# Metaformer kernel, first stage: in every second pair of rows ScalarE puts the mask into the gate and VectorE takes the pair's product in one operation

## The reference, cut to what matters

```python
m = mask[..., None]
a = _ln_fp32(act, ln_in_w, ln_in_b)
left  = m * (a @ left_proj_w.T  + left_proj_b)  * sigmoid(a @ left_gate_w.T  + left_gate_b)
right = m * (a @ right_proj_w.T + right_proj_b) * sigmoid(a @ right_gate_w.T + right_gate_b)
t = einsum('bikc,bjkc->bijc', left, right)
t = _ln_fp32(t, ln_c_w, ln_c_b)
out = (t @ out_proj_w.T + out_proj_b) * sigmoid(a @ gating_w.T + gating_b)
```

## Time and profile before

| | |
|---|---|
| median of 3 runs | 995.27 us (994.14 to 995.28) |
| the profiled execution's own time | 994.61 us |
| its span, first to last instruction | 992.8 us |
| mean granted TensorE clock over the span | 0.969 |
| busy over the span: TensorE matmul | 921.4 us (93%) |
| VectorE | 819.0 us (82%) |
| GpSimd | 660.1 us (66%) |
| ScalarE | 449.4 us (45%) |
| the first stage's products (L838) | 512 of them, started between 28.5 and 215.5 us |
| the first stage's sigmoids (L492) | 128 of them, started between 25.5 and 214.0 us |

### The profile page before, as it was taken

The page is one execution under the profiler, slowest core; times in us unless marked ns, Lnnn a source line. Parts: engine busy times, 40 slices in busy tenths (PEclk is TensorE's granted clock), DMA queues, the critical chain, the costliest instruction groups (busy, mean ns, idle before and its releaser), DMA issues.

```text
span 992.8 us, 22220 instructions
## 1 busy us (share of the span) xinstructions
PE 921.4 (93%) x7352; PEld 524.8 (53%) x7352; DVE 819.0 (82%) x2945; ACT 449.4 (45%) x842; POOL 660.1 (66%) x632
## 2 busy tenths in 40 slices
PE   4788999979999867999999999999999999999987
PEld 3566666758888544444444444444444444444432
DVE  4899999971122568999999999999999999999993
ACT  1555555641111123454554555545555455454543
POOL 5898888813322213877778777787777777877765
PEclk9999999989999955999999999999999999999999
DMA  7587777997997112324334333343342433433332
GB/s 195 179 283 246 265 264 261 311 351 235 306 300 228 32 32 76 107 90 125 114 100 128 98 117 120 96 128 103 112 127 88 128 112 104 125 97 120 102 93 73
DMA packets 119395, 153.15 MB, mean 154 GB/s; under 512 B 10486, under 2 KB 76278, under 8 KB 117238
## 3 DMA queue, kind: packets, MB, share of 16 engines
q1 hardware_dynamic: 118150, 151.32, 49.3%
q10 hardware_dynamic: 1136, 0.46, 0.2%
HBM read 67.33 MB, written 50.33 MB: 119 GB/s over the span
## 4 chain that ended last, share of the span: by engine, by line
PE 52%; DVE 35%; issue 6%; POOL 3%; DMA 3%; ACT 1%; SPq 0%; DVEq 0%; ACTq 0%; POOLq 0%
PE b_m L777 14%; PE ein L665 11%; DVE zb L1001 8%; DVE stage L838 7%; PE ring L764 6%; PE pr_a L628 4%; PE gt L702 4%; DVE bst L825 4%; PE gt L686 3%; PE b_d L686 3%; PE b_d L746 2%; DVE x2t L1020 2%; PE b_m L769 2%; DVE bst_x L1052 2%; DVE bst_t L899 2%
## 5 line engine op out<-in xcount | busy, mean ns | idle before, releaser
L442 POOL TENSOR_TENSOR zb<-bcs,x2d 128x512 f32<-128x512 f32 x256 | 326.3, 1277 | 154.3 <-ACT bcs L549 154.0
L549 ACT ACTIVATE bcs<-ring 128x512 f32<-128x512 f32 x256 | 152.7, 597 | 243.4 <-PE ring L764 243.3
L777 PE MATMUL b_m<-zb,w_exp 128*64 128x512 f32 x1024 | 253.7, 611 | 0.1
L1001 DVE TENSOR_TENSOR zb<-ring,x2d 128x512 f32<-128x512 f32 x256 | 175.5, 685 | 20.7 <-PE ring L764 18.6
L838 DVE SCALAR_TENSOR_TENSOR stage<-pr_a,mt,sig_a 128x128 f32<-128x128 f32 x512 | 148.4, 427 | 11.5 <-ACT sig_a L492 10.3
L628 PE MATMUL pr_a<-w_proj,xts 64*128 64x256 f32 x1024 | 138.2, 400 | 16.3 <-DVE stage L838 15.7
L777 PEld LDWEIGHTS b_m<-zb,w_exp 128*64 128x64 f32 x1024 | 61.0, 136 | 143.4 <-issue 118.3
L764 PE MATMUL ring<-wt,sel 64*128 64x512 f32 x512 | 127.5, 494 | 8.4 <-DVE zb L1001 4.4
L427 POOL TENSOR_TENSOR tn<-t_all,rr 128x512 f32<-128x512 f32 x64 | 85.3, 1333 | 52.0 <-DVE rr L929 27.4
L628 PEld LDWEIGHTS pr_a<-w_proj,xts 64*128 64x128 f32 x1024 | 95.5, 190 | 44.4 <-issue 26.1
L492 ACT ACTIVATE sig_a<-pr_a 128x512 f32<-128x512 f32 x128 | 76.4, 597 | 73.0 <-PE pr_a L628 72.8
(11 more groups left out here) (132 smaller groups left out, 1440.9 us busy)
## 6 DMA issues: line engine op xcount, KB each, us to landing
left_right_scratch<-stage SPq DMA_DIRECT2D x16, 2048.0 KB, 7.6
x2d<-x2t SPq DMA_DIRECT2D x256, 128.0 KB, 2.9
chunk<-left_right_scratch SPq DMA_DIRECT2D x24, 1024.0 KB, 9.1
xc<-in_x SPq DMA_DIRECT2D x64, 256.0 KB, 3.3
out<-outc SPq DMA_DIRECT2D x64, 256.0 KB, 2.1
chunk<-left_right_scratch SPq DMA_DIRECT2D x12, 384.0 KB, 7.6
chunk<-left_right_scratch SPq DMA_DIRECT2D x8, 192.0 KB, 5.9
chunk<-left_right_scratch SPq DMA_DIRECT2D x4, 256.0 KB, 8.0
```

The costliest lines, as they stand in the source:

```text
L442: pool.tensor_tensor(zb[:, tile_buffer(u, m), :], bcs[:, n % 2, :], x2d[:, u % 2, m % 2, :], ALU.mult)\
L549: act.activation(bcs[:, n % 2, :], ring[:, m % 2, :], ACT.Copy).then_inc(bcast_out, 1)
L777: ins = pe.matmul(b_m[rows[t], :], w_exp[:, ep, :], zb[:, tile_buffer(u, 2 * ep + t), :], start=ep == 0, stop=ep == EP - 1, skip_group_che ...
L1001: dve.tensor_tensor(zb[:, tile_buffer(u, m), :], ring[:, m % 2, :], x2d[:, u % 2, m % 2, :], ALU.mult).then_inc(z_dve, 1)
```

## The change

`act_masks(p)` is true for odd p. In such a pair ScalarE, after the sigmoid, waits for it on a new semaphore and then multiplies the mask into the gate in place, with four ACTIVATEs (Copy, with a per-partition scale read from `mt`), one for each row and q, of 128 elements. Only then is the gate announced to VectorE, which takes the product of projection and masked gate for the whole pair in one TENSOR_TENSOR of 512 elements in place of four SCALAR_TENSOR_TENSORs of 128. Even pairs are as before. The number of announcements on every semaphore that others wait for is unchanged.

```diff
+def act_masks(p):
+
+    return p % 2 == 1
...
-        sig_ready = sem("sig_ready"); lr_done = sem("lr_done"); stored = [sem("stored0"), sem("stored1")]
+        sig_ready = sem("sig_ready"); sig_raw = sem("sig_raw"); lr_done = sem("lr_done"); stored = [sem("stored0"), sem("stored1")]
...
                 if p >= PAIR_RING:
                     act.wait_ge(lr_done, p - PAIR_RING + 1)
-                act.activation(sig_a[:, k, :, :, :], pr_a[:, k, :, :].rearrange("p q (r c) -> p q r c", r=PAIR)[:, :, :, 2 * C:4 * C],
-                               ACT.Sigmoid).then_inc(sig_ready, 1)
+                gate_in = pr_a[:, k, :, :].rearrange("p q (r c) -> p q r c", r=PAIR)[:, :, :, 2 * C:4 * C]
+                ins = act.activation(sig_a[:, k, :, :, :], gate_in, ACT.Sigmoid)
+                if act_masks(p):
+                    ins.then_inc(sig_raw, 1)
+                    act.wait_ge(sig_raw, p // 2 + 1)
+                    for r in range(PAIR):
+                        for q in range(Q):
+                            row = p * PAIR + r
+                            ins = act.activation(sig_a[:, k, q, r, :], sig_a[:, k, q, r, :], ACT.Copy, scale=mt[:, row:row + 1, q])
+                ins.then_inc(sig_ready, 1)
...
                 if n >= 2 and p * PAIR % ROWS == 0:
                     dve.wait_ge(stored[n % 2], n // 2 * 16)
+                if act_masks(p):
+                    row = p * PAIR % ROWS
+                    ins = dve.tensor_tensor(
+                        stage[:, n % 2, :, :, row:row + PAIR].rearrange("p q c r -> p q r c"),
+                        pr_a[:, p % PAIR_RING, :, :].rearrange("p q (r c) -> p q r c", r=PAIR)[:, :, :, 0:2 * C],
+                        sig_a[:, p % PAIR_RING, :, :, :], ALU.mult)
+                    ins.then_inc(lr_done, 1)
+                    return
                 for r in range(PAIR):
```

## The result

The changed kernel is a little slower: 998.76 us median (997.49 to 1000.61, 6 runs) against 994.10 (993.38 to 995.28, 6 runs), a ratio of 1.0046 with a 95% interval of 1.0035 to 1.0056. That is +4.7 us where 3.4 us less was forecast: inside the stated range, on the other side of no change. The profiled execution took 998.70 us, its span is 996.9.

What follows compares the result with a forecast made beforehand. VectorE was taken to bound 30 groups and TensorE 31, with ScalarE the next limit. Terms -13.2, +9.3 and +0.5 gave -3.4 us: 991.2 from the profiled 994.61, 991.9 as median; range 981 to 1007.

Steps and rivals of the forecast that it cites:

- The phases and who sets them: First stage: VectorE sets groups with statistics at 3.29 us, TensorE those without at 2.51; ScalarE is late next everywhere.
- 30 groups for VectorE and 31 for TensorE: First stage, a group being two pairs with transposes: 30 gain, 3.29 to 2.85 us; 31 pay, 2.51 to 2.81.
- VectorE's part: Odd pair's products joined into one of 512 elements: 1.09 to 0.61 us, saving 0.48 a group.
- I take 0.61: Pace in us assumed for the 512-element product, as for close writes, between bounds of 0.61 and 1.05.
- A VectorE group: Two pairs with statistics beside them, set by VectorE: 3.29 us to 2.80, or 2.85 with 0.04 added for waits.
- The rival that the strided write holds the product: Long product's write, 64 bytes between neighbours, keeps it at 1.05 us: VectorE saves nothing, +9.8 us, 1005.1; chance 0.10.
- slower copies: ScalarE's four copies without overlap, 0.39 us each: its group is 3.22, total +21.3 us, 1016.6; chance 0.14.
- ScalarE's part: Evacuation 0.50, even sigmoid 0.50, odd sigmoid and wait 0.66, four copies at 0.287: 2.81 us a group.
- Its sum by that page, -1.9 us: Whole-time forecast with the skill page's estimated 0.294 us copy pace and a 2.84 us ScalarE group, instead of -3.4.
- The end, +0.5: Last, odd pair up to the contraction: ScalarE 1.2 us more, VectorE 0.45 less; 0.75 or nothing, taken as +0.5.
- At 22.7 a super block it still fits: GpSimd's work on each super block's statistics, 21.2 us, was claimed to fit the forecast super block.
- Stores and clock: Block stores nearly all fit and granted clock stays 1.00: both costed nothing; rival of 11.6 us stores +4, 999.3, chance 0.06.

Runs made afterwards that it cites:

- const_scale: The changed kernel with the four copies' scale a constant 1.0 instead of the mask pointer, mask left out in odd pairs; 0.9978 of the kernel before, -1.8 us.
- inner_rows: The changed kernel with the long product going through its elements with the two rows innermost, results placed as before; 0.9981 of the kernel before, -1.5 us.
- dve_inner: The changed kernel with the long product's two rows innermost and no ScalarE copies, mask left out in odd pairs; 0.9895 of the kernel before, -10.2 us.
- act_only: The changed kernel with VectorE's four short products kept in odd pairs beside ScalarE's copies, mask applied twice; 1.0105 of the kernel before, +10.1 us.
- stat_pairs: The changed kernel with ScalarE's mask only in odd pairs with statistics beside them, write order as in the change; 0.9982 of the kernel before, -2.0 us.
- stat_inner: The changed kernel with rows innermost in the long product and ScalarE's mask only in odd pairs with statistics; 0.9908 of the kernel before, -9.2 us.

## Why the prediction was wrong

- **The phases and who sets them: right.** 30 groups for VectorE and 31 for TensorE, a gain in the first and a price in the second; ScalarE late next. The last two super blocks show the price as described, 2.76 a group. Only TensorE's idleness does not show in its busy time, which is 23.46 of 24 us there and was 23.34; it covers 176 matmul records instead of 188.
- **VectorE's part: the step that failed.** "I take 0.61", since of the short product's pace of 0.263 nothing but 0.02 seemed left for the stride. The long product takes 0.86 of pace and 1.045 of length. The error was to take the stride's price from a pace: 0.06 of the 0.08 us that the write costs a short product lies under the start of the next one, and four short products hide it four times, a long one once. Their length had it all along: 427 ns where the 128-element product of 280 and 0.05 for a pointer make 330. Close writes made it 340. A VectorE group became 3.18 where 2.85 was forecast: 30 x 0.33 = 9.9 us, more than the whole miss of 4.7 + 3.4 = 8.1. The rival that the strided write holds the product went the right way and too far: it gave back all of the saving, and 0.11 to 0.18 of the 0.48 remained. The total lies in the stated range because the range took in this rival and slower copies; the forecast itself had the sign wrong.
- **ScalarE's part: right in size.** Forecast 0.287 pace, 0.06 wait, 2.81 a group; measured 0.297, 0.03, 2.76 (198.15 - 197.68 = 0.47 for the evacuation). Pointer in full: shown by const_scale. The pace that the prediction estimated from the Trainium skill, ScalarE: Activation LUTs, What ACT_TABLE_LOAD costs, was 0.294; the trace agrees within 0.003. Its sum by that page, -1.9 us, should read -1.7: 4 x 0.007 x 61 = 1.7 us above -3.4.
- **The sum with the measured groups**: 30 x (3.18 - 3.29) + 31 x (2.76 - 2.51) = -3.3 + 7.75 = +4.4, and the contraction starts 4.4 us later. The end, +0.5, is nearly hidden: the last product ends 4.9 us later (219.80 + 1.03 in the chain against 211.51 + 4.37), the contraction starts only 4.4 later.
- **GpSimd, costed at nothing, was not nothing.** "At 22.7 a super block it still fits" holds in the steady part: in inner_rows, at 22.91 a super block, GpSimd waits 1.7 us for statistics each time. But TensorE waits for its rows at 49 us, and the first five groups can give nothing. In the change this hides little, as little was to be gained; in dve_inner ten groups gave 1.6 us instead of 4.3.
- **The seam** was not seen either: 0.28 us a super block in act_only and 0.58 in stat_pairs and stat_inner, from VectorE's wait for the first copies after each phase without statistics. No run isolates it.
- Stores and clock: at nothing, and nothing came. The granted clock is 1.00 throughout the stage's steady part. VectorE's wait for a store was 1.2 us before and at most 0.2 after (2.0 of idle time before L859, 1.8 of it for ScalarE).

## What to carry to other kernels

A pace can hide a cost that its length shows: before short operations are joined into a long one, compare their length with one of close writes, and look for the order of elements that puts two results side by side. A change that shifts work from one engine to another pays only in the phase that the first engine sets; apply it there alone. Here the same idea went from +4.7 to -9.2 us by the order of two loops and the choice of 30 of 64 pairs.

## What had not been expected of the hardware

A 512-element product with one write to each 64 bytes takes 1047 ns, with two side by side in each 64 bytes 697, with all side by side 691. Reads that jump 1 KB in PSUM and 512 bytes in SBUF at every element cost nothing beside it (the same 697). The cost is 0.63 to 0.70 ns a written element in length. Of a 128-element product's 0.08 us all but 0.02 lies under the start of the next one; of a 512-element product's 0.36 us, 0.26 remain.
